# Cross-attention with a routed expert layer: the context laid out in runs of 6 KB, and its fourth part also laid out turned and loaded

## The chip, the core and the metric

The kernel runs on one core of a Trainium2 chip. The metric is the device time in microseconds (us) of one execution of the whole program. Its engines are TensorE (PE; PEld is its weight load), VectorE (DVE), ScalarE (ACT), GpSimd (POOL) and SyncE (SP), which here only issues transfers. Transfers run on 16 DMA engines that all queues share.

## The reference, cut to what matters

```python
def _L0_xattn_ref(hidden_states, memory_tokens, memory_mask):
    scores = jnp.einsum('bsd,bmd->bsm', hidden_states, memory_tokens) * scale
    scores = jnp.where(memory_mask[:, None, :], scores, neg_inf)
    attn = jax.nn.softmax(scores, axis=-1)
    readout = jnp.einsum('bsm,bmd->bsd', attn, memory_tokens)
    ...
def _L0_ffn_ref(x, Wg, W, b):
    probs = jax.nn.softmax(jnp.einsum('bsh,he->bse', x, Wg), axis=-1)
    onehot = jax.nn.one_hot(jnp.argmax(probs, axis=-1), E, dtype=x.dtype)
    y = jnp.einsum('bsh,ehd->bsed', x, W) + b
    return jnp.einsum('bsed,bse->bsd', y, onehot * probs)
x = x + jnp.tanh(g_xattn[0]) * _L0_xattn_ref(_layernorm(x), ctx_2048, mask_BxS2_bk0)
x = x + jnp.tanh(g_ffn[0]) * _L0_ffn_ref(_layernorm(x), Wg, W, b)
```

There are 32 batches of 112 tokens of 512 numbers (`x`), each with a context of 375 rows of 512 (`ctx_2048`), and 8 experts of 512 by 512. All numbers are float32.

## The kernel before

The program has two stages. In the **batch stage** each of the 32 batches goes through layer norm, scores, softmax, read-out, residual and the choice of an expert for each token; each finished row goes to `mid_rows` in memory, and an entry to `token_list`. In the **tile stage** 35 tiles of 128 tokens that chose the same expert are gathered, multiplied and scattered. The change is in the batch stage.

There is no scheduler. Each engine has its instructions written out by hand, and its `batch(i)` works on several batches at once. PE's `batch(i)` takes, in this order: the scores of batch i+1 (`scores`, L1104 to L1108), the turn of batch i's weights (`turn_weights`, L1116), parts 0 and 1 of the turn of context i+2 (`ctx_turn`, L1082), the ranks of batch i-2 (L1127, L1128), the first third of the read-out of batch i (`read_out`, L1141 and L1142), the turn of the normalised x of i+2 (`x_turn`, L1091), parts 2 and 3 of the turn of context i+2, and the other two thirds of the read-out.

A context of 375 rows lies in SBUF on 125 partitions of 3 rows (MC = 3 chunks). To multiply by it, PE turns it, 128 of its 512 columns at a time: these are the parts k = 0 to 3, each of three transposes into one of two PSUM banks. Of parts 0 to 2, ACT writes the value as fp32r (`ctxT_hi`, L630) and DVE the rest (`ctxT_lo`, L968); part 3 ACT copies in full float32 (`ctxT_full`, L632), and PE multiplies it in one full-precision product (L1107).

In `ctx_sb` the room ahead of each context row takes the turned weights and eight columns of the router (`SE` = 112 + 8). ACT writes both with one copy (`turned_weights`, L680), and `read_out` multiplies the 112 by the 8 with the 512 beside them, so that the router's product comes out with the read-out. Since the room is not loaded, the load of a context writes and reads runs of 512 numbers, 2 KB each: one DMA for partitions 0 to 111 (L368) and one for the other 13 (L369).

SP issues per batch i: the weights of i+2 (`w_raw`, L373) once POOL has split those of i+1; the finished rows to `mid_rows` (L398) once DVE has written `x2` (L824); and then x (L366) and context (L368, L369) of batch i+4. All of these run in order on one queue. POOL issues the scatter to `token_list` (L520) on another.

A circle through the other engines belongs to this stage: x_turn, ACT's `xnT_hi` (L687), DVE's `xnT_lo`, `xnT_full` and last `ctxT_lo`, its statistics of the next x (L769, L778), POOL's `stats1` (L478 to L488), ACT's `xn` (L695), `lexp` (L712) and `turned_weights` (L680), for which PE's `read_out` waits before the next x_turn.

Of the kernel before, what the change touches and what calls it, by code (L numbers as in the profile page):

```python
# [17 lines left out]
F32 = mybir.dt.float32  # L18
# [9 lines left out]
P = 128  # L28
# [79 lines left out]
def build(nc, x, ctx, mask, small, w_exp, b_exp, out):  # L108
# [37 lines left out]
    with ExitStack() as stack:  # L146
# [43 lines left out]
        ctx_sb = sb("ctx_sb", [P, 4 * MC, SE + D])  # L190
# [6 lines left out]
        ctxT_full = sb("ctxT_full", [P, MG])  # L197
# [55 lines left out]
        rows, biases, res = x_sb, ctx_sb[:, 0:E, SE:], ctx_sb[:, E:E + 4, SE:]  # L253
# [28 lines left out]
        ctx_ld = [sem(f"ctx_ld{i}") for i in range(4)]  # L282

# [18 lines left out]
        xnT_hi_ok, xnT_full_ok, ctxT_full_ok = sem("xnT_hi_ok"), sem("xnT_full_ok"), sem("ctxT_full_ok")  # L302
# [61 lines left out]
        def _(sp):  # L364
            def load(j):
                sp.dma_start(x_sb[0:S, j.slot(4), :], x_rows[bass.ds(j.times(S), S), :]).then_inc(x_ld[j.slot(4)], 16)  # L366
                rows_of = ctx[bass.ds(j.times(1), 1), :, :].rearrange("o (p c) d -> p (o c) d", c=MC)
                sp.dma_start(ctx_sb[0:MAIN, chunks(j), SE:], rows_of[0:MAIN, :, :]).then_inc(ctx_ld[j.slot(4)], 16)  # L368
                sp.dma_start(ctx_sb[MAIN:MP, chunks(j), SE:], rows_of[MAIN:MP, :, :]).then_inc(ctx_ld[j.slot(4)], 16)  # L369
# [23 lines left out]
            def batch(i):  # L393
# [49 lines left out]
        def _(pool):  # L443
# [174 lines left out]
        def _(act):  # L618
# [79 lines left out]
            def batch(i):  # L698
# [33 lines left out]
                if soon.within(B):  # L732
                    ctx_part(soon, 3)
# [19 lines left out]
        def _(dve):  # L753
# [42 lines left out]
            def center_router():  # L796
# [13 lines left out]
                dve.tensor_copy(ctxT_full[:, ME:MG], wg_mid[:, KS, :]).then_inc(wg_ok, 1)  # L810
# [131 lines left out]
            def read_counts(late):  # L942
                dve.wait_ge(count_mm, late + 1)
                dve.wait_ge(prT_ok, B if late else TAIL + 1)
# [20 lines left out]
            def low_part(j, k):  # L965

                dve.wait_ge(ctxT_hi_ok, j.times(KS, k + 1))
                dve.tensor_tensor(ctxT_lo[:, k, 0:M], ctx_ps[k % 2][:, 0:M], ctxT_hi[:, k, 0:M].bitcast(F32), ALU.subtract  # L968
# [101 lines left out]
        def _(pe):  # L1070
            def ctx_turn(j, k):
# [3 lines left out]
                if k >= 2:  # L1075
                    pe.wait_ge(ctxT_ok, j.times(KS, k - 1))
                elif k == 1 and j.at_least(1):
                    pe.wait_ge(ctxT_full_ok, j.times(1))
                elif j.at_least(1):
                    pe.wait_ge(ctxT_ok, j.times(KS))  # L1080
# [14 lines left out]
            def scores(j):  # L1095
# [5 lines left out]
                pe.wait_ge(ctxT_full_ok, j.times(1, 1))  # L1101
# [5 lines left out]
                pe.matmul(score_ps[a][0:SE, 0:MG], xnT_full[:, :], ctxT_full[:, :], start=False, stop=False)  # L1107
# [197 lines left out]
```

## Time and profile before

| | |
|---|---|
| time before, median of 3 runs | 391.55 us (391.52 to 391.95) |
| the profiled execution, its time | 394.58 us |
| its span, first to last instruction | 392.8 us |
| PE busy | 359.2 us (91%) |
| DVE, POOL, ACT busy | 301.0, 226.8, 220.6 us |
| mean granted TensorE clock | 0.976 of 2.4 GHz |
| packets and data moved | 39438, 67.21 MB |

The profiled execution is 3.0 us longer than the median of the runs, and 1.8 us of its time lie outside the span. PE's busy share is an average over both stages, and a matmul counts as busy from its start to its modelled end, so that a full PE can still be waited for by others. The DMA share is the time that packets took over that of 16 engines; a packet that hangs counts too, so a share near 1 with few GB/s is a stall and one with many is work.

### The profile page before, as it was taken

Reading aid. Unit: us, or ns where it says so; the run is one execution under the profiler, and the core shown is the slowest. Engines: PE = TensorE matmul, PEld = TensorE weight load, DVE = VectorE, ACT = ScalarE, POOL = GpSimd, SP = SyncE. Lnnn points to the kernel's source line nnn. Section 1 sums busy time; section 2 is a strip of 40 time slices with the busy share of each in tenths; the row PEclk is TensorE's granted clock in tenths of the full one; section 3 lists DMA queues with packets and bytes.
Section 4 is the critical chain, followed back from the end, with each engine's and each line's share of the span. In section 5 each row is a group of like instructions: output and inputs, shape, how many; then the busy total and the mean of one; then the engine's idle time right before and its main releaser. Section 6 shows DMA issues by size and latency. Waiting matters only on the chain.

```text
span 392.8 us, 9753 instructions
## 1 busy us (share of the span) xinstructions
PE 359.2 (91%) x2062; PEld 302.1 (77%) x2063; DVE 301.0 (77%) x1087; ACT 220.6 (56%) x488; POOL 226.8 (58%) x482
## 2 busy tenths in 40 slices
PE   7799999999999999999999999376999999999980
PEld 6688888878888888888888877255777878878760
DVE  4668888889898899889899988446877767767660
ACT  3577777777777677767777665132434444444410
POOL 5154675665666666665675654726466666666631
PEclk9999999999999999999999999968999999999995
DMA  7978789888989888899999861754345444445410
GB/s 197 222 188 222 179 196 221 194 199 204 202 203 197 206 193 217 201 188 220 198 201 234 196 152 52 164 179 135 110 158 158 141 146 145 129 149 158 153 37 0
DMA packets 39438, 67.21 MB, mean 171 GB/s; under 512 B 10578, under 2 KB 11094, under 8 KB 39416
## 3 DMA queue, kind: packets, MB, share of 16 engines
q1 hardware_dynamic: 32600, 50.35, 54.7%
q0 software_dynamic: 6624, 16.58, 13.2%
q8 instruction: 8, 0.13, 0.1%
q14 instruction: 14, 0.11, 0.1%
q10 hardware_dynamic: 192, 0.03, 0.0%
HBM read 51.68 MB, written 17.10 MB: 175 GB/s over the span
## 4 chain that ended last, share of the span: by engine, by line
PE 52%; DMA 16%; issue 9%; DVE 7%; POOL 6%; ACT 3%; SPq 3%; POOLq 1%; DVEq 1%; ACTq 0%
DMA ctx_sb<-in_ctx 8%; PE read_both L1141 8%; PE ctx_ps L1082 8%; PE read_both L1142 7%; DMA x_sb<-mid_rows,take 6%; PE score_ps L1180 4%; PE score_ps L1107 3%; POOL out_rows L590 3%; PE score_ps L1182 3%; PE score_ps L1181 3%; PE score_ps L1104 3%; PE score_ps L1105 3%; PE score_ps L1106 3%; PE prob_ps L1091 2%; PE ctx_ps L1162 2%
## 5 line engine op out<-in xcount | busy, mean ns | idle before, releaser
L1141 PE MATMUL read_both<-ctx_sb 125*112 125x264 f32 x192 | 61.1, 400 | 1.9 <-DVE lg L837 1.6
L1180 PE MATMUL score_ps<-w_hi,ctxT_hi 128*128 x140 | 59.7, 426 | 1.6 <-DVE ctxT_lo L908 1.6
L968 DVE TENSOR_TENSOR ctxT_lo<-ctx_ps,ctxT_hi 128x375 fp32r<-128x375 f32 x96 | 49.3, 541 | 13.2 <-ACT ctxT_hi L630 12.6
L520 POOL DMA_INDIRECT token_list<-pay,pos x32 | 32.2, 1007 | 46.2 <-DVE pos L889 41.1
L1142 PE MATMUL read_both<-ctx_sb 125*112 125x256 f32 x192 | 57.1, 379 | 0.0
L1082 PE MATMUL ctx_ps<-ident,ctx_sb 125*128 125x125 f32 x384 | 52.6, 272 | 4.4 <-DMA ctx_sb<-in_ctx 2.6
L1182 PE MATMUL score_ps<-w_lo,ctxT_hi 128*128 x140 | 56.4, 403 | 0.0
L1181 PE MATMUL score_ps<-w_hi,ctxT_lo 128*128 x140 | 56.3, 402 | 0.0
L581 POOL DMA_INDIRECT x_sb<-mid_rows,take x35 | 34.4, 982 | 29.8 <-DVE ctx_sb L926 17.9
L590 POOL DMA_INDIRECT out_rows<-ctx_sb,put x35 | 40.0, 1144 | 17.5 <-issue 9.4
L641 ACT ACTIVATE w_raw<-x_sb,li 128x512 f32<-128x512 f32 x35 | 28.5, 815 | 36.9 <-DMA x_sb<-mid_rows,take 36.9
L1082 PEld LDWEIGHTS ctx_ps<-ident,ctx_sb 125*128 125x128 f32 x384 | 42.4, 141 | 7.0 <-DMA ctx_sb<-in_ctx 2.7
L630 ACT ACTIVATE ctxT_hi<-ctx_ps 128x375 fp32r<-128x375 f32 x96 | 42.6, 481 | 4.9 <-PE ctx_ps L1082 4.9
L695 ACT ACTIVATE xn<-x_sb,ln 112x512 f32<-112x512 f32 x32 | 26.0, 814 | 33.3 <-POOL ln L484 33.3
L654 ACT ACTIVATE ctxT_hi<-ctx_ps 128x512 fp32r<-128x512 f32 x35 | 20.9, 598 | 40.6 <-PE ctx_ps L1162 40.6
L469 POOL TENSOR_TENSOR w_lo<-w_raw,w_hi 128x512 f32 (+1 forms) x32 | 40.8, 1275 | 0.0
L1142 PEld LDWEIGHTS read_both<-ctx_sb 125*112 125x112 f32 x192 | 34.0, 177 | 8.7
L1104 PE MATMUL score_ps<-ctxT_hi,xnT_hi 128*120 128x384 f32 x96 | 37.9, 395 | 1.8 <-DVE ctxT_lo L968 1.8
L921 DVE SCALAR_TENSOR_TENSOR x_sb<-ctx_sb,li,x_sb 128x512 f32<-128x512 f32 x35 | 26.3, 752 | 13.1 <-issue 12.8
L908 DVE TENSOR_TENSOR ctxT_lo<-ctx_ps,ctxT_hi 128x512 fp32r<-128x512 f32 x35 | 24.2, 691 | 15.1 <-ACT ctxT_hi L654 15.0
L1141 PEld LDWEIGHTS read_both<-ctx_sb 125*112 125x112 f32 x192 | 29.3, 176 | 5.3 <-ACT ctx_sb L680 2.3
L926 DVE SCALAR_TENSOR_TENSOR ctx_sb<-score_ps,li,x_sb 128x512 f32<-128x512 f32 x35 | 26.3, 751 | 8.7 <-PE score_ps L1182 7.7
(141 smaller groups left out, 828.2 us busy)
## 6 DMA issues: line engine op xcount, KB each, us to landing
ctx_sb<-in_ctx SPq DMA_DIRECT2D x32, 672.0 KB
w_raw<-in_L_ffn_W SPq DMA_DIRECT2D x32, 256.0 KB, 5.1
x_sb<-in_x SPq DMA_DIRECT2D x32, 224.0 KB, 4.4
mid_rows<-x SPq DMA_DIRECT2D x32, 224.0 KB, 3.4
ctx_sb<-in_ctx SPq DMA_DIRECT2D x32, 78.0 KB
ctx_sb<-in_L_ffn_b SPq DMA_DIRECT2D x8, 256.0 KB, 7.6
li<-token_list SPq DMA_DIRECT2D x35, 2.0 KB, 1.9
x_sb<-mid_rows,take POOLq DMA_INDIRECT x35, 3.4
```

The lines of the kernel that those rows point to most:

```text
L469: pool.tensor_tensor(w_lo[:, bass.ds(w.times(D), D)], w_raw[:, w.slot(2), :], w_hi[:, bass.ds(w.times(D), D)].bitcast(F32), ALU.subtract). ...
L581: pool.indirect_dma_start(rows[:, b, :], None, source, bass.IndirectOffsetOnAxis(take[:, b:b + 1], 0)).then_inc(row_ld[b], 16)
L590: pool.indirect_dma_start(out, bass.IndirectOffsetOnAxis(put[:, b:b + 1], 0), res[:, b, :], None, bounds_check=N - 1, oob_is_err=False).th ...
L630: act.activation(ctxT_hi[:, k, 0:M], ctx_ps[k % 2][:, 0:M], ACT.Copy).then_inc(ctxT_hi_ok, 1)
L968: dve.tensor_tensor(ctxT_lo[:, k, 0:M], ctx_ps[k % 2][:, 0:M], ctxT_hi[:, k, 0:M].bitcast(F32), ALU.subtract).then_inc(ctxT_ok, 1)
L1082: last = pe.transpose(ctx_ps[k % 2][:, c * MP:(c + 1) * MP], ctx_sb[0:MP, MC * j.slot(4) + c, SE + k * P:SE + (k + 1) * P], ident[0:MP, 0:MP])
L1104: pe.matmul(score_ps[a][0:SE, 0:MG], xnT_hi[:, k, :], ctxT_hi[:, k, :], start=(k == 0), stop=False)
L1141: pe.matmul(read_a, turned[:, 0:S], turned[:, S:SE + HALF], start=(c == 0), stop=(c == MC - 1))
L1142: last = pe.matmul(read_b, turned[:, 0:S], turned[:, SE + HALF:], start=(c == 0), stop=(c == MC - 1))
L1180: pe.matmul(y_ps[a][:, :], hi, w_hi[:, chunk], start=(k == 0), stop=False)
L1181: pe.matmul(y_ps[a][:, :], lo, w_hi[:, chunk], start=False, stop=False)
L1182: last = pe.matmul(y_ps[a][:, :], hi, w_lo[:, chunk], start=False, stop=(k == KC - 1))
```

## The change

The host lays out the context anew. Ahead of each row it puts eight zeros, the room of the router's columns, so that a row is 520 numbers in memory and in `ctx_sb`, and the three rows of a partition are one run of 1560 numbers (6240 bytes). The last 128 columns are also laid out turned, as 128 rows of 375, in a tensor of its own, `in_ctx_turned`; SP loads them into `ctxT_full`, which gets four slots. Part 3 of the turn and ACT's copy of it go. The turned weights get a tile of their own (`turned`), so ACT's one copy becomes two. Core of the diff:

```diff
-        ctx_sb = sb("ctx_sb", [P, 4 * MC, SE + D])
+        ctx_sb = sb("ctx_sb", [P, 4 * MC, E + D])
+        turned = sb("turned", [P, 2, MC * S])
...
-        ctxT_full = sb("ctxT_full", [P, MG])
+        ctxT_full = sb("ctxT_full", [P, 4, MG])
...
-                sp.dma_start(ctx_sb[0:MAIN, chunks(j), SE:], rows_of[0:MAIN, :, :]).then_inc(ctx_ld[j.slot(4)], 16)
-                sp.dma_start(ctx_sb[MAIN:MP, chunks(j), SE:], rows_of[MAIN:MP, :, :]).then_inc(ctx_ld[j.slot(4)], 16)
+                sp.dma_start(ctx_sb[0:MAIN, chunks(j), :], rows_of[0:MAIN, :, :]).then_inc(ctx_ld[j.slot(4)], 16)
+                sp.dma_start(ctx_sb[MAIN:MP, chunks(j), :], rows_of[MAIN:MP, :, :]).then_inc(ctx_ld[j.slot(4)], 16)
+
+            def load_turned(j):
+                sp.dma_start(ctxT_full[:, j.slot(4), 0:M], ctx_t[bass.ds(j.times(1), 1), :, :].rearrange("o d m -> (o d) m")
+                             ).then_inc(ctxT_ld[j.slot(4)], 16)
...
                     load(i.plus(4))
+                    sp.wait_ge(score_mm, i.times(1, 1))
+                    load_turned(i.plus(4))
...
-                act.wait_ge(ctxT_mm, j.times(4, k + 1))
+                act.wait_ge(ctxT_mm, j.times(KS, k + 1))
...
-                if k < KS:
-                    act.activation(ctxT_hi[:, k, 0:M], ctx_ps[k % 2][:, 0:M], ACT.Copy).then_inc(ctxT_hi_ok, 1)
-                else:
-                    act.activation(ctxT_full[:, 0:M], ctx_ps[k % 2][:, 0:M], ACT.Copy).then_inc(ctxT_full_ok, 1)
+                act.activation(ctxT_hi[:, k, 0:M], ctx_ps[(j.at + k) % 2][:, 0:M], ACT.Copy).then_inc(ctxT_hi_ok, 1)
...
-                if j.at_least(4):
-                    act.wait_ge(read_mm, j.times(1, -3))
-                act.activation(ctx_sb[0:MP, chunks(j), 0:SE],
-                               prob_ps[0:MP, 0:MC * SE].rearrange("p (c s) -> p c s", c=MC), ACT.Copy).then_inc(prT_ok, 1)
+                if j.at_least(2):
+                    act.wait_ge(read_mm, j.times(1, -1))
+                both = prob_ps[0:MP, 0:MC * SE].rearrange("p (c s) -> p c s", c=MC)
+                act.activation(turned[0:MP, j.slot(2), :].rearrange("p (c s) -> p c s", c=MC), both[:, :, 0:S], ACT.Copy
+                               ).then_inc(prT_ok, 1)
+                act.activation(ctx_sb[0:MP, chunks(j), 0:E], both[:, :, S:SE], ACT.Copy).then_inc(prT_ok, 1)
...
-                pe.wait_ge(ctxT_full_ok, j.times(1, 1))
+                pe.wait_ge(ctxT_ld[j.slot(4)], j.rounds(4) * 16 + 16)
...
-                    pe.wait_ge(prT_ok, j.times(1, 1))
+                    pe.wait_ge(prT_ok, j.times(2, 2))
...
-                pe.matmul(read_a, turned[:, 0:S], turned[:, S:SE + HALF], start=(c == 0), stop=(c == MC - 1))
+                weight, values = turned[0:MP, a, c * S:(c + 1) * S], ctx_sb[0:MP, MC * j.slot(4) + c, :]
+                pe.matmul(read_a, weight, values[:, 0:E + HALF], start=(c == 0), stop=(c == MC - 1))
...
                     ctx_turn(turned, 2)
-
-                    ctx_turn(turned, 3)
```

With three parts a batch, the two PSUM banks alternate from batch to batch (`(j.at + k) % 2`), and `ctx_turn` waits for `ctxT_lo` of the part two before it. The wait of SP on `score_mm` is for the scores of batch i, which are behind `x2` of batch i, for which SP has waited before.

PE in the loop of the batch stage, before, from the first third of the read-out to the second (`ctx_ps` are the turned parts, `prob_ps` the turned x):

```order
L1141 MATMUL read_both<-ctx_sb 112x264
L1142 MATMUL read_both<-ctx_sb 112x256
L1088 REGISTER_ALU
L1091 MATMUL prob_ps<-ident,xn 128x112 x4
L1076 REGISTER_ALU
L1082 MATMUL ctx_ps<-ident,ctx_sb 128x125 x3
L1076 REGISTER_ALU
L1082 MATMUL ctx_ps<-ident,ctx_sb 128x125 x3
L1141 MATMUL read_both<-ctx_sb 112x264
```

The same place now:

```order
L1147 MATMUL read_both<-ctx_sb,turned 112x264
L1148 MATMUL read_both<-ctx_sb,turned 112x256
L1094 REGISTER_ALU
L1097 MATMUL prob_ps<-ident,xn 128x112 x4
L1086 REGISTER_ALU
L1088 MATMUL ctx_ps<-ident,ctx_sb 128x125 x3
L1147 MATMUL read_both<-ctx_sb,turned 112x264
```

One group of three transposes is gone, behind x_turn; what stands ahead of x_turn is the same.

ACT in the loop, before, from the normalised x to the softmax's first rows (`ctx_sb<-prob_ps` is `turned_weights`):

```order
L695 ACTIVATE xn<-x_sb,ln 112x512
L712 ACTIVATE lexp,lsum<-lsh,pay 112x8
L679 REGISTER_ALU
L680 ACTIVATE ctx_sb<-prob_ps 125x3x120
L626 REGISTER_ALU
L630 ACTIVATE ctxT_hi<-ctx_ps 128x375
L626 REGISTER_ALU
L630 ACTIVATE ctxT_hi<-ctx_ps 128x375
L687 ACTIVATE xnT_hi<-prob_ps 128x3x112
L626 REGISTER_ALU
L630 ACTIVATE ctxT_hi<-ctx_ps 128x375
L731 ISA
```

The same place now:

```order
L706 ACTIVATE xn<-x_sb,ln 112x512
L723 ACTIVATE lexp,lsum<-lsh,pay 112x8
L690 ACTIVATE turned<-prob_ps 125x336
L692 ACTIVATE ctx_sb<-prob_ps 125x3x8
L638 REGISTER_ALU
L641 ACTIVATE ctxT_hi<-ctx_ps 128x375
L638 REGISTER_ALU
L641 ACTIVATE ctxT_hi<-ctx_ps 128x375
L698 ACTIVATE xnT_hi<-prob_ps 128x3x112
L638 REGISTER_ALU
L641 ACTIVATE ctxT_hi<-ctx_ps 128x375
L742 ISA
```

The second copy stands ahead of the two `ctxT_hi`; the removed copy of part 3 stood behind these rows.

SP in the loop, one batch, before (ISA rows carry addresses):

```order
L373 DMA w_raw<-in_L_ffn_W 128x512
L398 ISA
L398 DMA mid_rows<-x 112x512
L366 ISA
L366 DMA x_sb<-in_x 112x512
L368 ISA
L368 DMA ctx_sb<-in_ctx 112x3x512
L369 ISA
L369 DMA ctx_sb<-in_ctx 13x3x512
```

The same batch now:

```order
L379 DMA w_raw<-in_L_ffn_W 128x512
L408 ISA
L408 DMA mid_rows<-x 112x512
L368 ISA
L368 DMA x_sb<-in_x 112x512
L370 ISA
L370 DMA ctx_sb<-in_ctx 112x1560
L371 ISA
L371 DMA ctx_sb<-in_ctx 13x1560
L374 ISA
L374 DMA ctxT_full<-in_ctx_turned 128x375
```

A sixth transfer stands behind the context and ahead of the next batch's `w_raw`.

## Rows read from the trace of the kernel before

**Rows 1.** The page: span, busy time by engine, and the span in 40 slices.
```profile
span 392.8 us, 9753 instructions
PE 359.2 (91%) x2062; PEld 302.1 (77%) x2063; DVE 301.0 (77%) x1087; ACT 220.6 (56%) x488; POOL 226.8 (58%) x482
...
PE   7799999999999999999999999376999999999980
...
DMA  7978789888989888899999861754345444445410
```

**Rows 2.** The chain that ended last: start us, us, what.
```profile
28.18 0.64 PE ctx_ps L1082 x6
...
35.36 0.64 PE ctx_ps L1082 x6
...
42.52 0.64 PE ctx_ps L1082 x6
...
57.49 0.64 SPq L368
58.32 6.14 DMA ctx_sb<-in_ctx
64.51 0.86 PE ctx_ps L1082 x6
...
234.36 0.64 PE ctx_ps L1082 x6
```

**Rows 3.** Waits, whole span: us in total, times, longest.
```profile
ACT xn L695 <- POOL ln L484: 33.3, 32, 2.6
...
PEld ctx_ps L1082 <- DMA ctx_sb<-in_ctx: 2.7, 5, 1.0
PE ctx_ps L1082 <- DMA ctx_sb<-in_ctx: 2.6, 4, 0.9
```

**Rows 4.** The chain between 152 and 162 us: start us, us, what.
```profile
154.16 0.54 DVE ctxT_lo L968
...
156.11 1.00 POOL token_list L520
...
158.75 0.20 POOL ln L484
...
159.70 0.32 ACT lexp L712 x2
160.01 0.06 ACT ctx_sb L680
...
161.31 0.54 DVE ctxT_lo L968
```

**Rows 5.** Groups with shapes apart: count | busy us, mean ns of one | idle before.
```profile
L1082 PE MATMUL ctx_ps<-ident,ctx_sb 125*128 125x125 f32 x384 | 52.6, 272 | 4.4 <-DMA ctx_sb<-in_ctx 2.6 <-DVE ctxT_lo L968 1.7
L630 ACT ACTIVATE ctxT_hi<-ctx_ps 128x375 fp32r<-128x375 f32 x96 | 42.6, 481 | 4.9 <-PE ctx_ps L1082 4.9
...
L654 ACT ACTIVATE ctxT_hi<-ctx_ps 128x512 fp32r<-128x512 f32 x35 | 20.9, 598 | 40.6 <-PE ctx_ps L1162 40.6
...
L632 ACT ACTIVATE ctxT_full<-ctx_ps 128x375 f32<-128x375 f32 x32 | 15.7, 491 | 0.0
```

**Rows 6.** ACT in order of time, one batch: start us, us, what, idle before.
```profile
108.75 0.19 ACT L712 ACTIVATION_READ_ACCUMULATOR lexp<-lsh,pay 112x1 f32 x1
108.93 0.47 ACT L680 ACTIVATE ctx_sb<-prob_ps 125x360 f32<-125x360 f32 x1
109.30 0.48 ACT L630 ACTIVATE ctxT_hi<-ctx_ps 128x375 fp32r<-128x375 f32 x1
```

**Rows 7.** PE in order of time, the same place.
```profile
109.45 0.70 PE L1141 MATMUL read_both<-ctx_sb 125*112 125x264 f32 x2
```

**Rows 8.** Stretches: from:to and length us, then PEclk, DMA share, GB/s.
```profile
3.00:4.00 1.00, 1.00 0.75 164
...
22.00:22.50 0.50, 1.00 1.08 310
25.25:27.00 1.75, 1.00 0.02 5
60.00:220.00 160.00, 1.00 0.89 204
160.25:161.75 1.50, 1.00 0.89 68
163.25:166.00 2.75, 1.00 1.06 234
...
171.00:171.50 0.50, 1.00 1.00 356
```

More of the change, by code:

```diff
@@ L105, in run, with build @@
         body(Count(n))
-def build(nc, x, ctx, mask, small, w_exp, b_exp, out):
+def build(nc, x, ctx, ctx_t, mask, small, w_exp, b_exp, out):
     B, S, D = x.shape
@@ L250, in build @@
         put = sb("put", [P, 4], U32)
-        rows, biases, res = x_sb, ctx_sb[:, 0:E, SE:], ctx_sb[:, E:E + 4, SE:]
+        rows, biases, res = x_sb, ctx_sb[:, 0:E, E:], ctx_sb[:, E:E + 4, E:]
         rn = w_raw
@@ L282, in build @@
         ctx_ld = [sem(f"ctx_ld{i}") for i in range(4)]
+        ctxT_ld = [sem(f"ctxT_ld{i}") for i in range(4)]
         fill_st, zero_st = sem("fill_st"), sem("zero_st")
@@ L375, in _ @@
             load(Count(0))
+            load_turned(Count(0))
             sp.wait_ge(st1_ok, 1)
             load(Count(1))
+            load_turned(Count(1))
             load_w(Count(0))
@@ L383, in _ @@
             load(Count(3))
+            load_turned(Count(3))
             sp.wait_ge(fill_ok, 2)
@@ L943, in read_counts @@
                 dve.wait_ge(count_mm, late + 1)
-                dve.wait_ge(prT_ok, B if late else TAIL + 1)
+                dve.wait_ge(prT_ok, 2 * (B if late else TAIL + 1))
                 dve.tensor_scalar(cnt_i[:, :], count_ps, float(P - 1) if late else 0.0, None, ALU.add
@@ L967, in low_part @@
                 dve.wait_ge(ctxT_hi_ok, j.times(KS, k + 1))
-                dve.tensor_tensor(ctxT_lo[:, k, 0:M], ctx_ps[k % 2][:, 0:M], ctxT_hi[:, k, 0:M].bitcast(F32), ALU.subtract
+                dve.tensor_tensor(ctxT_lo[:, k, 0:M], ctx_ps[(j.at + k) % 2][:, 0:M], ctxT_hi[:, k, 0:M].bitcast(F32), ALU.subtract
                                   ).then_inc(ctxT_ok, 1)
@@ L1074, in ctx_turn @@
                     pe.wait_ge(ctx_ld[j.slot(4)], j.rounds(4) * 32 + 32)
-                if k >= 2:
+                if k >= 2 or j.at_least(1):
                     pe.wait_ge(ctxT_ok, j.times(KS, k - 1))
[L1077 to L1080, printed above, removed]
                 for c in range(MC):
-                    last = pe.transpose(ctx_ps[k % 2][:, c * MP:(c + 1) * MP],
-                                        ctx_sb[0:MP, MC * j.slot(4) + c, SE + k * P:SE + (k + 1) * P], ident[0:MP, 0:MP])
+                    last = pe.transpose(ctx_ps[(j.at + k) % 2][:, c * MP:(c + 1) * MP],
+                                        ctx_sb[0:MP, MC * j.slot(4) + c, E + k * P:E + (k + 1) * P], ident[0:MP, 0:MP])
                     if c == MC - 1:
@@ L1138, in read_out @@
                         pe.wait_ge(gv_ok, 1)
-                turned = ctx_sb[0:MP, MC * j.slot(4) + c, :]
-                pe.matmul(read_a, turned[:, 0:S], turned[:, S:SE + HALF], start=(c == 0), stop=(c == MC - 1))
-                last = pe.matmul(read_b, turned[:, 0:S], turned[:, SE + HALF:], start=(c == 0), stop=(c == MC - 1))
+                weight, values = turned[0:MP, a, c * S:(c + 1) * S], ctx_sb[0:MP, MC * j.slot(4) + c, :]
+                pe.matmul(read_a, weight, values[:, 0:E + HALF], start=(c == 0), stop=(c == MC - 1))
+                last = pe.matmul(read_b, weight, values[:, E + HALF:], start=(c == 0), stop=(c == MC - 1))
                 if c == MC - 1:
@@ L1295 @@
         a = _np.ascontiguousarray(inputs[name])
+        room = inputs["L0_ffn_b"].shape[0]
+        if name == "ctx_2048":
+            last = a[:, :, a.shape[2] - 128:].reshape(a.shape[0], a.shape[1] // 3, 3, 128).transpose(0, 3, 2, 1)
+            last = _np.ascontiguousarray(last.reshape(a.shape[0], 128, a.shape[1]))
+            a = _np.concatenate([_np.zeros(a.shape[:2] + (room,), a.dtype), a], axis=2)
         if name == "L0_ffn_W":
@@ L1299 @@
         args.append(nc.dram_tensor(f"in_{name}", a.shape, _mybir.dt.from_np(a.dtype), kind="ExternalInput").ap())
+        if name == "ctx_2048":
+            arrays["in_ctx_turned"] = last
+            args.append(nc.dram_tensor("in_ctx_turned", last.shape, _mybir.dt.from_np(last.dtype), kind="ExternalInput").ap())
     b, s, d = inputs["x"].shape
```

12 lines of the change are left out of this document (6 added, 6 removed).

## The prediction

> **What bounds the kernel now.** I read the page first. PE is at 9 tenths or more in nearly every slice of the batch stage, and DVE and the DMA engines are not far behind [rows 1]. A page like that names several candidates and decides nothing, so the chain of waits comes next. In quiet rounds it stays on PE: the first transposes of a context start at 28.18, 35.36 and 42.52 us, one round in 7.18 and 7.16 us. Between 57.49 and 64.51 us it leaves PE: SP issues a context load, the data land 6.14 us later, and PE takes up the transposes 0.05 us behind that. From 28.18 to 234.36 us are 28 rounds, so one takes 7.36 us on average [rows 2]. So 7.17 is the floor of a round, and 0.19 us a round, 5.4 us in all, is what late transfers and their echoes add. PE or its weight load waited for a context 9 times [rows 3].
>
> Is PE alone that floor? The chain between 152 and 162 us says no. It goes from ctxT_lo on DVE (154.16) over POOL's token_list and ln to ACT's lexp (159.70), ACT's turned weights (160.01) and back to ctxT_lo (161.31): a round of 7.15 us without PE [rows 4]. ACT waits for POOL's ln in all 32 batches, 1.04 us each [rows 3], so its own work elsewhere in the round is free, and the stretch from ln to the read-out is not. In the round at 108 us ACT's lexp ends at 108.94, the turned weights start at 108.93 and end at 109.40 [rows 6], and PE's read-out starts at 109.45 [rows 7]. Two circles of the same length, one through PE and one through ACT, DVE and POOL, meet at that read-out. The second takes from PE only what lies between the read-out's first third and the end of x_turn.
>
> The transfers are the third limit. From 60 to 220 us the 16 DMA engines show a share of 0.89 at 204 GB/s. That share has two kinds of time in it: 356 GB/s at a share of 1.00 (171.00 to 171.50), and 68 GB/s at 0.89 (160.25 to 161.75), where the stores of rows and tokens hang [rows 8].
>
> **PE's part.** Six transposes take 0.64 us on the chain [rows 2], so three take 0.32 us. That is what a round of PE loses, about 10 us over 32 batches. (The 272 ns that each shows in [rows 5] overlap.) Two things stand against it. The three stood behind x_turn, so the other circle does not contain them. And the read-out now waits for ACT's second copy.
>
> **ACT's part.** The copy of part 3, 491 ns [rows 5], goes. ACT waits 1.04 us a batch for POOL anyway, so this pays nothing. The second copy has 24 numbers a partition. From 375 to 512 numbers a copy goes from 481 to 598 ns [rows 5], 0.85 ns a number, so one of 24 takes some 0.18 us; consecutive copies overlap by 0.10 us (109.30 against an end of 109.40) [rows 6]. So the read-out is released some 0.08 us later; the ends are 0.03 us (the first copy being 24 numbers shorter) and 0.18 us (no overlap). PE's circle becomes 7.17 - 0.32 + 0.08 = 6.93 us. The other had between 0 and 0.1 us of room at the copy and becomes 7.15 to 7.25. I take 7.17: the floor stays. If the circle had 0.2 us of room, the floor would be 7.05.
>
> **The transfers' part.** A batch's context becomes 12 KB larger and 192 KB come with the turned part, behind the context and ahead of w_raw, on the one queue of SP. So 204 KB more go past the next weights, stores, x and context. Nothing in the trace has runs of over 2 KB on SP's queue. What run length is worth I take from two stretches: fills in runs of 1 KB at 310 GB/s and a share of 1.08, and context loads in 2 KB runs at 356 and 1.00 [rows 8]. Over 16 engines that is 57 ns for 1 KB and 92 ns for 2 KB, so 22 ns fixed and 35 ns for each KB. A run of 6240 bytes then takes 235 ns and replaces three of 92: 41 ns less, 125 runs on 16 engines, -0.32 us a batch. A turned row of 1500 bytes takes 73 ns, 8 rows an engine, +0.59 us. Net +0.27 us. The bounds: if in the crowded stretch (234 GB/s at 1.06) only bytes count, 204 KB at 221 GB/s are +0.92 us. If long runs bring the whole context from today's 229 GB/s (204 over 0.89), 3.35 us, to the clean 356, 2.19 us, then it is -1.16 + 0.59 = -0.57 us. I take +0.27, since it comes from the rows nearest in kind.
>
> Here the rows and a page part. In these stretches the time of a transfer depends on the length of its runs, 287 against 356 GB/s at full share. The Trainium skill, "DMA: Bandwidth & Descriptors", section "Anatomy of one DMA", fits a transfer as some 2 us plus its bytes over 436 GB/s, and its "Specifications" ask of a run only 512 bytes for line rate. By that page the 6 KB runs give nothing and 204 KB cost an estimated 0.47 us a batch. That speaks against the change; it is the third rival below.
>
> **What the 0.27 us do to the end.** The 9 waiting rounds get all of it, 2.4 us. Some 8 more, which land just in time, I charge with half, 1.1 us. The other rounds hide it. At the start, the first context load is supplied too slowly to fill the engines (164 GB/s at a share of 0.75 from 3 to 4 us [rows 8]); fewer and longer runs should bring it in by 0.32 us, and SP's two issues behind it take less time, so -0.6 us. The three further turned loads of the start add 0.6 MB, which the idle stretch of 1.75 us before 27 us (5 GB/s [rows 8]) takes up. SP's new wait costs nothing: it is for scores that lie behind an x2 for which SP already waited. Nothing in the tile stage changes but strides. The sum: 2.4 + 1.1 - 0.6 = +2.9 us. The profiled execution, at 394.58 us, is 3.0 above the median of 391.55; the same difference on the median gives **394.4 us**.
>
> **Rivals.**
> First, **long runs carry**. It is the bound of -0.57 us: context loads land early, the 0.19 us a round go, 28 x 0.19 = 5.4, and with the start 391.5 - 5.4 - 0.6 = 385.5 us; with a floor of 7.05 it is 382. For it: most of the context's time today passes in the crowded stretches, whose cause I can't read. Against: if they are crowded by bytes, longer runs don't help there.
> Second, **it comes out even**. The stall of 1.5 us at 160 us [rows 8] ends when slow stores end, whatever the queue does, so that work behind it can slip into the stall. Then only the start remains: 391.0 us, within 0.2%.
> Third, **bytes alone**: 0.47 us more a batch, the 9 rounds get 4.2, 8 others half, 1.9, less 0.6: 397 us. I count it in the slower case.
> Fourth, **the queue never catches up**. At +0.92 us the queue's work per round passes 7.36 + 0.92 less some 0.3 of room: +0.6 us in 28 rounds, 17 us, 408 us. It decides once the added time is more than the idle time left in a round, some 0.3 us.
> Fifth, **the PE saving counts in full**: if the other circle had over 0.3 us of room, the rounds that don't wait for transfers, 19 of them, would gain 0.24 each, 4.6 us, 389.8 us with the forecast's transfers. The room that [rows 6] show speaks against it.
>
> **How the numbers follow.** The forecast, slower by 392.3 to 400 us, has 0.42, and the queue that never catches up 0.06. Even has 0.16. Long runs, with the PE saving in part, have 0.36, from 382 to 390.8. What a measurement of this kernel can tell from no change is about 0.2%, 0.8 us. So slower by more than that is 0.48, within 0.16, faster 0.36. The range leaves out the 408 case and the lower edge of the fast one: 384 to 399.5. The likeliest case's own range is 392.3 to 399.5.
>
> **What would show it.** In the profile after, the step on PE is right if rounds without a wait stay at 7.1 to 7.2 us although PE's busy time falls by some 10 us, with PE's read-out waiting for ACT's second copy. The step on ACT is right if that copy takes 0.15 to 0.2 us and the read-out starts 0.05 us behind its end. The step on the transfers is right if q1 moves 6.5 MB more, its share rises, and contexts land about as late as now, 6 to 7 us from issue. The forecast is wrong if contexts land in under 5.5 us (long runs carry), if quiet rounds take less than 7.05 us (the other circle had room), or if w_raw is waited for.

## The result and the profile after

The changed kernel takes 396.13 us (median of 4 runs, 394.84 to 397.0) against 391.53 us for the kernel before in the same series (4 runs, 390.46 to 391.95): a ratio of 1.0114, 95% interval 1.0075 to 1.0154. It is 1.1% slower. The forecast was 394.4.

The profiled execution after takes 394.84 us. It lies 1.3 us under its median, and that of the kernel before lay 3.0 us over its own, so the two traces are nearly equally long (spans of 393.0 and 392.8 us). They show where time moved; how much the change costs only the medians say. The profiled execution is also the fastest of its four.

The page after, first its span and busy times, then SP's queue and landing times (the last number of a DMA row is the median from issue to landing, in us):

```profile
span 393.0 us, 9635 instructions
...
PE 353.2 (90%) x1966; PEld 292.2 (74%) x1967; DVE 301.5 (77%) x1087; ACT 208.7 (53%) x488; POOL 227.4 (58%) x482
...
q1 hardware_dynamic: 29208, 56.88, 58.5%
...
w_raw<-in_L_ffn_W SPq DMA_DIRECT2D x32, 256.0 KB, 5.7
x_sb<-in_x SPq DMA_DIRECT2D x32, 224.0 KB, 4.0
mid_rows<-x SPq DMA_DIRECT2D x32, 224.0 KB, 4.0
ctxT_full<-in_ctx_turned SPq DMA_DIRECT2D x32, 187.5 KB, 6.6
```

PE lost 6.0 us of busy time and ACT 11.9 us against [rows 1]. The stretch from 60 to 220 us, which was 0.89 at 204 GB/s before [rows 8], now (columns: from:to and length, busy us of each engine, PEclk, DMA share, GB/s):

```profile
60.00:220.00 160.00, 153.03 (x911) 129.74 (x910) 142.62 (x584) 106.61 (x281) 101.03 (x260) 1.00 0.95 231
```

The chain of waits after, first its beginning, then the first transposes of contexts 3, 4, 5, 8 and 31:

```profile
0.80 0.43 ACTq L631
1.23 0.03 issue
1.26 6.04 DMA small_sb<-in_small
7.30 0.02 issue
7.32 0.22 DVE wg_part L792
...
10.62 1.25 PE ctx_ps L1088 x6
...
30.89 0.64 PE ctx_ps L1088 x6
...
37.88 0.64 PE ctx_ps L1088 x6
...
44.88 0.64 PE ctx_ps L1088 x6
...
59.50 7.16 DMA ctx_sb<-in_ctx
66.77 0.85 PE ctx_ps L1088 x6
...
236.78 0.64 PE ctx_ps L1088 x6
```

Three things are to be seen. Quiet rounds take 6.99 and 7.00 us, not 7.17 as in [rows 2]. From context 3 to context 31 a round takes (236.78 - 30.89) / 28 = 7.35 us all the same, as before (7.36). And the loop starts 2.7 us later than at 28.18 [rows 2]: the chain now begins with the router's table `small_sb`, a DMA of 17 KB on ACT's queue that lands 6.04 us behind its issue. The waits for contexts have grown from 5.3 us in 9 waits [rows 3]:

```profile
ACT xn L706 <- POOL ln L496: 41.9, 31, 2.7
...
PE ctx_ps L1088 <- DMA ctx_sb<-in_ctx: 6.1, 10, 1.2
```

### The profile page after: what moved, and what is told of

Same layout as the page of the kernel before. It is cut to its first block, busy times and chain, and to the rows that moved or that the text cites. A ratio compares the mean times of both kernels' runs of the same rounds, so it can differ in the third digit from the quotient of the medians.

```text
span 393.0 us, 9635 instructions
## 1 busy us (share of the span) xinstructions
PE 353.2 (90%) x1966; PEld 292.2 (74%) x1967; DVE 301.5 (77%) x1087; ACT 208.7 (53%) x488; POOL 227.4 (58%) x482
## 4 chain that ended last, share of the span: by engine, by line
PE 47%; DMA 22%; DVE 11%; issue 9%; ACT 3%; SPq 3%; POOL 1%; DVEq 1%; POOLq 0%; ACTq 0%
DMA ctx_sb<-in_ctx 13%; PE score_ps L1186 7%; PE score_ps L1188 7%; PE score_ps L1187 7%; PE read_both L1147 5%; PE ctx_ps L1088 4%; DMA x_sb<-mid_rows,take 4%; PE read_both L1148 4%; DMA x_sb<-in_x 4%; PE ctx_ps L1168 4%; DVE st L778 2%; DVE x L834 2%; DVE ctxT_lo L978 2%; PE score_ps L1113 2%; PE prob_ps L1097 2%
## 5 line engine op out<-in xcount | busy, mean ns | idle before, releaser
L1147 PE MATMUL read_both<-ctx_sb,turned 125*112 125x264 f32 x192 | 60.9, 399 | 2.3 <-DVE lg L847 1.8
L1148 PE MATMUL read_both<-ctx_sb,turned 125*112 125x256 f32 x192 | 57.1, 379 | 0.0
L1088 PE MATMUL ctx_ps<-ident,ctx_sb 125*128 125x125 f32 x288 | 43.2, 278 | 8.1 <-DMA ctx_sb<-in_ctx 6.1
L1088 PEld LDWEIGHTS ctx_ps<-ident,ctx_sb 125*128 125x128 f32 x288 | 32.5, 144 | 11.6 <-issue 9.3
L1148 PEld LDWEIGHTS read_both<-ctx_sb,turned 125*112 125x112 f32 x192 | 34.0, 177 | 8.7
L1110 PE MATMUL score_ps<-ctxT_hi,xnT_hi 128*120 128x384 f32 x96 | 36.3, 378 | 2.9 <-DVE ctxT_lo L978 2.9
L1147 PEld LDWEIGHTS read_both<-ctx_sb,turned 125*112 125x112 f32 x192 | 29.2, 176 | 6.4 <-issue 2.2
L1111 PE MATMUL score_ps<-ctxT_hi,xnT_lo 128*120 128x384 f32 x96 | 32.4, 338 | 0.0
```

What stands on the lines that cost most here:

```text
L1088: last = pe.transpose(ctx_ps[(j.at + k) % 2][:, c * MP:(c + 1) * MP], ctx_sb[0:MP, MC * j.slot(4) + c, E + k * P:E + (k + 1) * P], ident[0 ...
L1110: pe.matmul(score_ps[a][0:SE, 0:MG], xnT_hi[:, k, :], ctxT_hi[:, k, :], start=(k == 0), stop=False)
L1147: pe.matmul(read_a, weight, values[:, 0:E + HALF], start=(c == 0), stop=(c == MC - 1))
L1148: last = pe.matmul(read_b, weight, values[:, E + HALF:], start=(c == 0), stop=(c == MC - 1))
```

## The experiments

The table has all of them. "Ctx 3" is when PE starts the first transposes of context 3, and "round" the mean round from there to context 31, by PE in order of time (the chain shows these starts 0.1 to 0.2 us later). "SP" is the time that the packets of SP's queue took, per batch and engine: q1's share times the span, over 32. The last four columns are of the one profiled execution; the median is of all executions, and the ratio is against the kernel before in the same series. A column of one execution is not exact to the last digit: e5 and e9, which differ in how the turned rows are laid out only, have rounds of 7.32 and 7.38 us.

| kernel | median us | ratio, 95% interval | ctx 0 | ctx 3 | round | SP |
|---|---|---|---|---|---|---|
| before | 391.5 to 392.1 | | 8.18 | 28.01 | 7.36 | 6.71 |
| after | 396.13 | 1.0114, 1.0075 to 1.0154 | 10.41 | 30.73 | 7.35 | 7.18 |
| e1 table first | 394.53 | 1.0070, 1.0037 to 1.0103 | 8.19 | 31.61 | 7.32 | 7.15 |
| e2 long runs only | 393.98 | 1.0063, 1.0034 to 1.0093 | 9.51 | 29.75 | 7.31 | 6.32 |
| e3 turned load only | 397.23 | 1.0159, 1.0114 to 1.0205 | 7.95 | 30.34 | 7.42 | 7.26 |
| e4 no reload | 391.19 | 0.9997, 0.9968 to 1.0027 | 11.16 | 32.89 | 7.18 | 6.43 |
| e5 table and fill | 392.50 | 1.0014, 0.9978 to 1.0050 | 8.83 | 29.30 | 7.32 | 7.16 |
| e6 before, table first | 392.72 | 1.0008, 0.9966 to 1.0049 | 8.46 | 29.00 | 7.37 | 6.61 |
| e7 e5, no reload | 388.42 | 0.9886, 0.9840 to 0.9931 | 8.10 | 27.80 | 7.22 | 6.50 |
| e8 one run | 387.63 | 0.9880, 0.9831 to 0.9930 | 7.11 | 26.60 | 7.16 | 5.63 |
| e9 aligned | 394.86 | 1.0081, 1.0055 to 1.0107 | 8.01 | 27.68 | 7.38 | 7.15 |
| e10 one context load | 387.70 | 0.9900, 0.9875 to 0.9925 | 6.91 | 26.56 | 7.14 | 5.67 |
| e11 one run alone | 390.36 | 0.9957, 0.9928 to 0.9986 | 8.38 | 29.44 | 7.17 | 5.60 |
| e12 one load, turned by PE | 391.65 | 0.9999, 0.9974 to 1.0024 | 7.39 | 27.31 | 7.30 | 5.13 |

**First series: which part costs what.** e1, the table issued first on SP's queue:

```diff
-            act.dma_start(small_sb[:, :], small).then_inc(small_ld, 16)
...
+            sp.dma_start(small_sb[:, :], small).then_inc(small_ld, 16)
```

> The changed kernel, with the router's small table (17 KB) issued by SP ahead of x and context of batch 0, where ACT issued it before. In the trace of the change the table lands 6.0 us after its issue against 2.6 before, DVE starts the router's sums at 7.32 us against 5.21, and the first transposes of a context start at 10.41 us against 8.18. Theory S (the start): the late table costs some 2.5 us of the 4.6 us lost; the first transposes return to 8.2 us or earlier and the time is 393.3 to 394.0 us. Rival L (the loop): the start is made up for by batch 8, since contexts then wait for transfers anyway; the time stays within 0.5 us of the change (395.6 to 396.6).

e2 has the layout of the change (rows of 520, runs of 6240 bytes, the weights in `turned`) and part 3 turned by PE as before:

```diff
-                sp.dma_start(ctx_sb[0:MAIN, chunks(j), SE:], rows_of[0:MAIN, :, :]).then_inc(ctx_ld[j.slot(4)], 16)
+                sp.dma_start(ctx_sb[0:MAIN, chunks(j), :], rows_of[0:MAIN, :, :]).then_inc(ctx_ld[j.slot(4)], 16)
```

> Half of the change: context rows of 520 numbers in runs of 6240 bytes with the two copies of ACT, but part 3 turned by PE and copied by ACT as before, and nothing loaded turned. Theory F (a fixed cost for each run, 22 ns): a batch's transfers take 0.3 us less, so that fewer contexts are late, while ACT's second copy adds 0.1 us to the circle and the table may land late: 391 to 393 us, quiet rounds at 7.2 us. Rival C (long runs carry): contexts land in 6.0 us or less, no round waits, under 388 us with the start as before. Rival B (bytes alone): transfers are as slow as before and the second copy and the late start remain, 394 us or more.

e3 is the changed kernel with the room of 120 columns and runs of 2 KB of the kernel before:

```diff
-        ctx_sb = sb("ctx_sb", [P, 4 * MC, E + D])
+        ctx_sb = sb("ctx_sb", [P, 4 * MC, SE + D])
```

> The other half: the fourth part of the context laid out turned and loaded, PE and ACT relieved of it, but the context in 2 KB runs as before and one copy of the turned weights. Theory F: the transfers take 0.6 us more a batch, nearly every round waits for its context, PE's 0.32 us are not seen: 396 to 399 us, the start as before. Rival P (the PE saving counts): rounds of 6.85 to 6.95 us, under 388 us. Rival B (bytes alone, 0.47 us a batch or less): 394 to 396 us.

e4 loads the turned part for the first four batches only, so later batches multiply by an old one:

```diff
-                    sp.wait_ge(score_mm, i.times(1, 1))
-                    load_turned(i.plus(4))
```

> The changed kernel, with the turned part loaded for the first four batches only; later batches multiply by those four in turn, so their scores are computed from other data. All instructions of PE, ACT, DVE and POOL stay, 28 transfers of 188 KB go. It shows the floor of a round without the added transfers. Theory T (transfers set the rounds of the change): rounds fall from 7.35 to 6.9 to 7.05 us, 386 to 389 us. Rival K (the circle over ACT's second copy, DVE and POOL sets them): rounds stay at 7.15 to 7.25 us, 391 to 393 us.

Measured, e1: by the medians the table first gives back 1.6 us (396.13 to 394.53), as PE's first transposes move from 10.41 to 8.19 us. That lies between its two expectations, and the intervals of the ratios of the changed kernel and e1 overlap, so that this gain is not clear of noise by itself. But context 3 is no earlier. Stretches of e1:

```profile
8.00:27.00 19.00, 15.41 (x70) 12.59 (x71) 8.66 (x24) 8.11 (x19) 3.85 (x15) 0.73 0.97 242
12.00:16.00 4.00, 4.00 (x11) 3.26 (x11) 0.28 (x2) 0.81 (x1) 1.19 (x5) 0.50 1.05 302
21.00:24.00 3.00, 3.00 (x9) 2.24 (x9) 0.72 (x4) 2.12 (x5) 2.21 (x6) 0.50 1.02 237
10.66:11.75 1.09, 0.00 (x1) 0.03 (x1) 0.99 (x4) 0.25 (x1) 0.00 (x0) 0.50 1.06 163
```

The granted clock is 0.50 in the last three, the lower level of 1.2 GHz: during the first two batches' scores, and already in the wait ahead of the first, which lasts from 10.40 to 11.75 us. PE in order of time in e1:

```profile
11.75 0.64 PE L1111 MATMUL score_ps<-ctxT_hi,xnT_hi 128*120 128x384 f32 x1 [1.35 <-DVE ctxT_lo L979]
12.19 0.52 PE L1112 MATMUL score_ps<-ctxT_hi,xnT_lo 128*120 128x384 f32 x1
```

The kernel before waited 0.90 us at this place, since part 3 lay in between, and its clock from 8 to 27 us was 1.00. Of the others the clock over the same stretch was 0.92 in e2 (where the low stretch lies ahead of the first scores), 0.82 in e3 and 0.91 in e11. In the row of the changed kernel it is 1.00 too, but there it can't be taken at its word: PE's first six transposes of a context took 1.46 us instead of the 0.83 of the kernel before and e1, so that PE worked at the lower level up to about 13 us, where the clock records of this trace begin. Then it waited as long as e1 and kept the higher level. First transposes and first scores of the changed kernel:

```profile
10.41 1.46 PE L1088 MATMUL ctx_ps<-ident,ctx_sb 125*128 125x125 f32 x6
...
14.61 0.41 PE L1110 MATMUL score_ps<-ctxT_hi,xnT_hi 128*120 128x384 f32 x1 [1.35 <-DVE ctxT_lo L978]
```

So of the 2.7 us by which its loop starts later, 2.2 are there when the first transposes start, by the late table, and some 0.6 come from the slow work between them and the first scores (4.20 us instead of 3.56). Its other executions have no trace.

Of the loop, the turned loads are the largest part: without them (e4) a round takes 7.18 us instead of 7.35 and the kernel 4.9 us less. By time and mean round that is what its rival K expected, but K had the reason wrong: the quiet rounds are 6.98 to 7.02 us, not 7.15 or more. Long runs come out at 0.07 us a round (e3's 7.42 against 7.35), which is no more than e5 and e9 differ by; e3's time fits its theory F, though its start was not as before (30.34 us). Without the shorter turn (e2) the quiet rounds take 7.23 us: the kernel before's 7.17 and 0.06 for the second copy. And PE waits for a context in e2 for 0.5 us in 2 waits only, where the kernel before waited 5.3 us in 9:

```profile
PEld ctx_ps L1085 <- DMA ctx_sb<-in_ctx: 0.5, 2, 0.3
```

So the long runs alone did take the late contexts away. What they gave (a round 0.05 us shorter, 1.5 us in all) the later start took back (context 3 at 29.75 us against 28.01), and the time of 393.98 us lies above the 391 to 393 of theory F, at the edge of rival B, whose reason the short waits refute.

**Second series: do the costs add up, and can the turned part come cheaper?** e5 is e1 with throwaway products in the gap:

```diff
                     ctx_turn(turned, 2)
+                    if at < 0:
+                        for n in range(16):
+                            pe.matmul(score_ps[at % 2][:, 0:P], ones_bf[:, :], ones_bf[:, :], start=True, stop=True)
```

> The changed kernel with the router's table first on SP's queue (as in e1) and, behind part 2 of the turn of contexts 0 and 1, 16 bf16 products of 128 by 128 on PE whose result nobody reads. They stand where PE otherwise waits 1.35 us for ctxT_lo ahead of the first two scores. If the removed transposes cost the start by letting TensorE's clock fall (e1: scores at 520 ns instead of 340 from 12.2 to 17.5 and from 20.8 to 24.3 us), the granted clock stays at 2.4 GHz there, the first transposes of context 3 start at 28.0 to 28.6 us instead of 31.6, and the time is 391.0 to 392.0 us, 3 us under e1's 394.5. Rival: the clock isn't the cause, or falls all the same; then context 3 starts at 31 us or later and the time stays at 394.5.

e6 is the kernel before with e1's edit:

> The kernel before with the router's table first on SP's queue instead of ACT's. In the kernel before, the table lands 2.6 us after its issue. If the late table is a cost of the change alone, this edit gives nothing or loses a little, since the first context is issued 0.1 to 0.4 us later: 391.3 to 392.3 us. Rival: the table on SP's queue is better whatever the context's layout, and this kernel comes to 390.0 us; then what e1 gained is no part of the change's cost.

e7 is e5 with e4's edit (an old turned part from the fifth batch on):

> As e5, but the turned part is loaded for the first four batches only and not again, so that later batches use an old one; its traffic is left out. If the three costs add up (the late table, the fallen clock, the turned loads), it takes e5's start and e4's loop of 7.18 us a round: 386.5 to 388.0 us, 4 us under e5. It is the price at which the shorter turn would pay in full. Rival: rounds of 6.9 us bring the context's load and the stores to the fore again, the loop stays at 7.18 or more and the start's gain is lost waiting for contexts in the first rounds: 389.5 to 391 us.

e8 lays the turned part behind the context rows:

```diff
-                sp.dma_start(ctx_sb[0:MAIN, chunks(j), :], rows_of[0:MAIN, :, :]).then_inc(ctx_ld[j.slot(4)], 16)
-                sp.dma_start(ctx_sb[MAIN:MP, chunks(j), :], rows_of[MAIN:MP, :, :]).then_inc(ctx_ld[j.slot(4)], 16)
...
-                sp.dma_start(ctxT_full[:, j.slot(4), 0:M], ctx_t[bass.ds(j.times(1), 1), :, :].rearrange("o d m -> (o d) m")
-                             ).then_inc(ctxT_ld[j.slot(4)], 16)
...
+                sp.dma_start(ctx_runs[:, j.slot(4), 0:RUN], ctx[bass.ds(j.times(1), 1), :, :].rearrange("o p n -> (o p) n")
+                             ).then_inc(ctx_ld[j.slot(4)], 16)
```

> As e5, but the turned part has no load of its own. The host lays 128 columns of it behind each of the three context rows of a partition, so that one load of 128 partitions, each a run of 7740 bytes, brings context and turned part: 128 runs instead of 253 and one DMA instead of three, at 18 KB more. By 22 ns a run the transfers lose 125 runs of 16 engines, 0.17 us a batch, which is what e4 showed the turned load to cost a round (7.35 against 7.18). If the number of runs matters, the loop comes to 7.18 to 7.25 us and the time to 387.5 to 389.5. Rival: bytes alone matter; then the context lands later, as the turned bytes now stand ahead of its end (7740 against 6240 bytes, some 0.4 us), and the time is 392 to 394.5.

The scores behind the fill run at the full clock (e5, 8 to 27 us):

```profile
8.00:27.00 19.00, 17.16 (x116) 14.80 (x114) 10.52 (x29) 10.30 (x23) 4.03 (x16) 1.00 0.95 246
```

And the time falls from 394.53 to 392.50, half a microsecond above the 391.0 to 392.0 that I had expected. The 1.00 of this row holds from the first scores on only. Context 3 starts at 29.30 and not at 28.0 to 28.6, for two reasons: in this execution the first context landed 0.6 us later, and PE worked at the lower level up to its first scores, as in the changed kernel:

```profile
8.83 1.48 PE L1089 MATMUL ctx_ps<-ident,ctx_sb 125*128 125x125 f32 x6 [0.60 <-DMA ctx_sb<-in_ctx]
```

The better witnesses are e7 and e9, which start as e5 does: their first six transposes take 0.83 us, the clock is 1.00 from there to 27 us and beyond, and context 3 starts at 27.80 and 27.68 us, where e1 had 31.61. So the two costs of the start are 3.6 us together, and with both mended the change is worth nothing either way. In the kernel before the table on SP's queue gains nothing (e6), so its delay is the change's own. e7 lost another 4.1 us, as e4 had: the turned load's price is the same with a good start, a little short of what I had expected (388.42 against at most 388.0).

e8 was the surprise. It loads 18 KB more than e5 and is 4.9 us faster. Its expectation came out, but by more than its reason: the queue's time a batch fell by 1.53 us (7.16 to 5.63), nine times the 0.17 that 125 fewer runs should give. Something else that e8 removed was expensive.

**Third series: what was it?** e9 aligns the turned rows, in e5:

```diff
-                sp.dma_start(ctxT_full[:, j.slot(4), 0:M], ctx_t[bass.ds(j.times(1), 1), :, :].rearrange("o d m -> (o d) m")
+                sp.dma_start(ctxT_full[:, j.slot(4), 0:ME], ctx_t[bass.ds(j.times(1), 1), :, 0:ME].rearrange("o d m -> (o d) m")
```

> As e5, but the rows of the turned part are 1536 bytes apart in memory instead of 1500 and 1504 bytes of each are loaded, so that each begins on a multiple of 512 bytes. In e8 the same bytes took 46.8% of the 16 engines' span against e5's 58.7%. If the unaligned rows of 1500 bytes are what costs there, the share of SP's queue falls from 58.7% to 50 to 53% and the time from 392.5 to 389 to 390 us. Rival: it is the number of runs and of DMAs; then the share stays within 1 point of 58.7% and the time at 392.0 to 393.0.

e10 joins the context's two DMAs, in e5:

```diff
-                sp.dma_start(ctx_sb[0:MAIN, chunks(j), :], rows_of[0:MAIN, :, :]).then_inc(ctx_ld[j.slot(4)], 16)
-                sp.dma_start(ctx_sb[MAIN:MP, chunks(j), :], rows_of[MAIN:MP, :, :]).then_inc(ctx_ld[j.slot(4)], 16)
+                sp.dma_start(ctx_sb[:, chunks(j), :], rows_of).then_inc(ctx_ld[j.slot(4)], 16)
```

> As e5, but the context is one DMA of 128 partitions of 6240 bytes (three of zeros) in place of one of 112 and one of 13; the turned part keeps its own load. If it is the small DMA of 13 runs that costs (its runs go to 13 engines behind everything else and it delays what is behind it), the time falls to 389 to 390 us and the share of SP's queue by 5 points or more. Rival: it is the turned part's own load of 128 short runs; then the time is 392.0 to 392.8 and the share above 57%.

e11 is the changed kernel with e8's layout and nothing else:

> e8 without its two edits at the start: the table goes back to ACT's queue and the throwaway products go; only the layout in one run of 7740 bytes differs from the changed kernel. By the difference of the changed kernel (396.1) and e5 (392.5) these two are worth 3.6 us: 391.2 us, with the table landing some 6 us from its issue and scores at 520 ns in the first batches. Rival: with one DMA instead of three the first context is out of the way sooner, the table lands in 3 us, and only the clock's part is lost: 388.5 to 389.5.

e12 is e2 with e10's edit and e1's:

> The kernel before with the context in runs of 6240 bytes as one DMA of 128 partitions, the turned weights in a tile of their own and the table first on SP's queue, but with part 3 still turned by PE and no turned load: e8 without what shortens PE's work. If the shorter turn is what e8's gain rests on, quiet rounds stay at 7.23 to 7.24 us as in e2, the loop at 7.26 or more, and the time is 390.0 to 392.0. Rival: the gain is all in the transfers and the start; then it comes within 1 us of e8's 387.6.

The third series has its answer in e10. It keeps the turned part's own load, and yet the queue's share falls by 11.6 points from e5's 58.7% and the time to e8's (387.70 us), below the 389 to 390 us that I had given to a costly DMA of 13 partitions. The page of e10:

```profile
span 385.4 us, 9621 instructions
...
q1 hardware_dynamic: 29032, 57.50, 47.1%
...
w_raw<-in_L_ffn_W SPq DMA_DIRECT2D x32, 256.0 KB, 3.8
x_sb<-in_x SPq DMA_DIRECT2D x32, 224.0 KB, 3.4
mid_rows<-x SPq DMA_DIRECT2D x32, 224.0 KB, 2.4
ctxT_full<-in_ctx_turned SPq DMA_DIRECT2D x32, 187.5 KB, 5.3
```

and its stretch from 60 to 220 us:

```profile
60.00:220.00 160.00, 158.40 (x948) 134.70 (x948) 147.57 (x607) 109.55 (x293) 104.92 (x273) 1.00 0.75 240
```

Against the same stretch of the changed kernel, more bytes (240 GB/s against 231) move in less engine time (0.75 against 0.95), and every other transfer, none of them edited, lands 0.6 to 1.9 us sooner. What went is one DMA of 13 partitions and one of 112, for one of 128. The same place in both kernels, while the first turned load moves; first e1, where it follows the DMA of 13 partitions:

```profile
5.75:6.75 1.00, 1.00 (x17) 0.90 (x16) 0.95 (x6) 0.52 (x1) 0.85 (x6) 1.00 1.01 143
```

then e10:

```profile
5.40:6.00 0.60, 0.60 (x8) 0.54 (x8) 0.38 (x3) 0.00 (x0) 0.49 (x1) 1.00 1.04 360
```

The engines are as full in both, and move 143 and 360 GB/s. But the DMA of 13 partitions is not all of it. From 4.50 to 5.25 us, e1 and then e10:

```profile
4.50:5.25 0.75, 0.38 (x7) 0.23 (x4) 0.72 (x5) 0.00 (x0) 0.26 (x2) 1.00 1.04 291
```

```profile
4.50:5.25 0.75, 0.49 (x9) 0.35 (x6) 0.72 (x5) 0.00 (x0) 0.22 (x2) 1.00 0.99 408
```

Up to 5.25 us e1 has moved 0.88 MB, and mask, table, x and the 112 partitions are 0.96 MB, so that by bytes the larger DMA is still under way here, and it is already slower than in e10. A load of 112 partitions is not slow by itself either: x is one, and from 2.75 to 3.10 us, where nearly nothing else moves, it goes at 334 GB/s in e1 and 328 in e10. So the pair is what costs, and which of the two does it stays open. Alignment is not it: e9's share stayed at 58.3%, and at 394.86 us it is even slower than e5 was in its series. Its trace has longer waits for contexts (8.5 us against 5.7), for which I have no reason.

The Trainium skill, "SBUF — State Buffer", section "Door 1: The DMA port swizzle", says that a transfer's rate depends on how many of 16 ports its partitions reach, and its formula puts partitions 112 to 124 on four of them. The Trainium skill, "DMA: Bandwidth & Descriptors", section "Rules for kernel authors", asks for 128 partitions a DMA and says not to bother with two transfers to disjoint partition halves. The traces agree with the second and go further, since the split not only gains nothing but costs (0.95 of the engines' time against 0.75). The first fits the slow 13 partitions, but no run here tells it from another reading, that the DMA of 112 partitions, 7 runs an engine, is slow with long runs. A kernel with two DMAs of 128 partitions each, and the kernel before with one, would tell; neither was run.

e11 shows what the start costs in this layout: 390.36 against e8's 387.63, 2.7 us, between the two expectations. The table lands 5.2 us behind its issue. The clock from 11.75 to 17 us is 0.67:

```profile
11.75:17.00 5.25, 5.19 (x22) 4.29 (x22) 0.79 (x3) 1.43 (x3) 1.19 (x5) 0.67 1.01 349
```

e12, which loads nothing turned, has the cheapest transfers of all and still takes 391.65 us, as expected, since PE turns part 3 and a round's floor is 7.23 us. So the two edits pay only together: the shorter turn alone (e5) 1.0014, the one load alone (e12) 0.9999, both (e10) 0.9900.

## Why the prediction was right or wrong

**The sign and the size** came out, the steps did not: two errors cancelled, so the near hit of 394.4 on 396.13 us is luck. The sum had +3.5 us in the loop and -0.6 at the start, +2.9 in all. The traces have -0.3 in the loop (28 rounds by -0.011 us) and +2.7 at the start, +2.4 in all. The stretch behind the last `x2` takes that back in the two traces: it took 140.8 us before and 138.4 after, and 135.6 to 140.6 in the other kernels, although nothing is edited there. So of the 4.6 us between the medians the traces place 2.4 us, and the rest is in no trace. Carrying a sum made on one execution over to a median was therefore good to some 3 us only, about as much as the sum itself. Nor can 0.2% be told from no change, as the prediction had it from three executions: 29 executions of the kernel before lie between 388.9 and 393.9 us, and the intervals of the ratios are 0.25 to 0.5% to either side.

**PE's part** was right: three transposes fewer, 0.32 us a round, 6.0 us of busy time in all, where I had said 10. The traces differ by 96 matmul records, three for each of 32 batches, so that missing records are not the reason.

**ACT's part** was right in its size. The second copy takes 0.17 us and read_out starts 0.06 us behind it. ACT, then PE, in order of time:

```profile
45.05 0.43 ACT L690 ACTIVATE turned<-prob_ps 125x336 f32<-125x336 f32 x1
45.38 0.17 ACT L692 ACTIVATE ctx_sb<-prob_ps 125x24 f32<-125x24 f32 x1
```

```profile
45.61 0.70 PE L1147 MATMUL read_both<-ctx_sb,turned 125*112 125x264 f32 x2
```

e2 puts its price at 0.06 us a round (7.23 against 7.17); I had said 0.08.

**The floor of 7.17 was wrong**, and it is the step that failed first. I read the circle through POOL as having 0 to 0.1 us of room because the chain ran through it for one round [rows 4] and ACT met PE closely at the read-out [rows 6, 7]. But the circle's round of 7.15 us had been timed by PE's own round: a follower shows its leader's period. The changed kernel has rounds of 6.88 to 7.0 us. The circle exists, as e10 shows once transfers no longer disturb. Most of its rounds take 6.99 to 7.11 us, with 7.02 the most frequent and every fourth at 7.27 or more, and the chain goes through the circle, here once in 7.07 us:

```profile
106.15 0.54 DVE ctxT_lo L978
...
108.35 0.07 POOL token_list L533
...
110.62 0.20 POOL ln L497
...
111.76 0.19 ACT lexp L723
...
112.18 0.17 ACT ctx_sb L692
...
113.22 0.54 DVE ctxT_lo L978
```

Its room was thus about 0.15 us, between the value I took and the 0.2 that I kept as the other end (a floor of 7.05). The rival "PE saving in full" wanted over 0.3; about 0.15 of its 0.24 are there.

**The transfers' part.** I had -0.32 us a batch for long runs, +0.59 for the turned part, +0.27 in all. In the queue's time, e2 measures -0.39 (6.71 to 6.32) and e3 +0.55 (6.71 to 7.26): both terms close to their estimates. Together they are +0.47 (6.71 to 7.18), not +0.16: the terms don't add. The estimate of 0.47 that the prediction works out from the Trainium skill's page, by bytes alone, is the same number, and e10 shows that this is chance: with more bytes still, its time is 1.04 below that of the kernel before. (The Trainium skill's page gives that fit for transfers that GpSimd issues, and these are SP's.) What I called the unreadable cause of the crowded stretches was the thing to ask about. I put 68 GB/s at a share of 0.89 [rows 8] down to stores that hang. The stores are the same in e10 and land in 2.4 us instead of 4.0 in the changed kernel and 3.4 in the kernel before. The scatter of POOL, from 60 to 220 us, after and then in e10 (5.5 us in the kernel before):

```profile
token_list<-pay,pos POOLq DMA_INDIRECT x22, 6.2
```

```profile
token_list<-pay,pos POOLq DMA_INDIRECT x22, 3.4
```

So they were victims more than the cause. How many rounds wait was right in kind: 10 waits for contexts on PE. On the chain contexts land 6.9 to 7.8 us from issue, later than the 6 to 7 that I expected.

**The start was wrong in sign.** I let the first context land earlier and named nothing that it could push back. The table, on another queue, is issued at the same moment as the context (1.26 us), and beside the long runs it landed in 6.04 us instead of the 2.6 of the kernel before. The added turned load is not the reason: with it and runs of 2 KB (e3) the table took 2.6 us, and without it and with long runs (e2) 5.5. SP also issues the context of long runs in 0.42 us and that of 2 KB runs in 0.73 us; what of the delay is the runs' length and what their earlier arrival no run tells. And I looked for what the removed transposes cost on the critical path, not for what they did for the clock while PE waited.

**The rivals.** "It comes out even" had the loop right by another road: the floor fell by 0.17 to 0.29 us and late contexts took it back. "Long runs carry" was right in e2 on the late contexts, but not on what they are worth, and in the changed kernel the turned loads bring the waits back. "The queue never catches up" falls with the loop of 7.35. "Bytes alone" at 397 us was near the time and is refuted as a reason by e8 and e10.

## What to carry to other kernels

Before a transfer is called limited by bytes, look at how it is split: here padding 125 partitions to 128, so that one DMA takes the place of 112 + 13, took the engines' share from 0.95 to 0.75 and 4.8 us off the kernel (e5 to e10). A circle that runs at another's period says nothing of its own length; only its waits, each round, show its room. And work taken off PE ahead of a wait in the first batches may be what kept the clock up: throwaway products in its place are cheap.

## What the runs showed of the hardware

A small DMA can be held up by what another queue moves: 17 KB took 6.04 us beside runs of 6240 bytes (5.5 in e2) and 2.6 beside runs of 2 KB (before, and e3). The share of busy DMA engines says little about bytes: 143 and 360 GB/s at a share just over 1. And where nothing fills the gap that part 3 left ahead of the first scores (a wait of 1.25 to 1.35 us), the clock fell to 1.2 GHz in that wait or up to 1.2 us behind it in e1, e3 and e11; with 16 throwaway products there (e7 to e10), and with part 3 in place and a wait of 0.90 us (before, e12), it stayed up from the first transposes to 27 us. In the traces of the changed kernel and of e4 PE came to the wait from the lower level; it got the higher one in the first and stayed at the lower in the second.
